# Context attention's softmax kept in its PSUM bank: scores plus side input written back, maxima and subtraction read there

## The chip, the cores and the metric

The kernel runs on one core of one Trainium2 chip. The metric is the device time of one execution in microseconds (us), the median of several runs. Durations of single instructions are in nanoseconds (ns) where marked.

## What is computed

Two layers on x of shape 4 x 1024 x 512, with a context of 4 x 64 x 512. The change lies in the first one, the attention over the context:

```python
qh = (q @ wq + bq).reshape(B, Lq, H, dk).transpose(0, 2, 1, 3)      # 16 heads of 64
kh = (k @ wk + bk).reshape(B, 64, H, dk).transpose(0, 2, 1, 3)
vh = (v @ wv + bv).reshape(B, 64, H, dv).transpose(0, 2, 1, 3)
scores = jnp.einsum('bhqd,bhkd->bhqk', qh / np.sqrt(dk), kh)
scores = scores + bias + graph_attn_bias        # both are the same input fside
weights = jax.nn.softmax(scores, axis=-1)       # over 64 context positions
ctx = jnp.einsum('bhqk,bhkd->bhqd', weights, vh)
out = layernorm(ctx @ wo + bo + q)
```

The second layer is a transformer block on that result: layer norm, self attention with 8-bit rounding of queries, keys, values and weights, attention over the context with the same rounding, and a gated feed-forward network of width 2048. Its code is not touched.

## The kernel before

The 4096 rows are worked on in eight chunks of 512 rows (n from 0 to 7), two chunks to a batch element; a chunk has NT = 4 tiles of 128 rows. For each batch element the kernel runs `cross` for both chunks, then `self_attention` and `middle` for each of them. The feed-forward network of a finished chunk is cut into 48 steps of twelve matmuls, and `feed` deals these out between the steps of later stages by hand-written plans; in `cross` of chunks 2 to 7 one such step comes ahead (slot 0) and the rest of that stage's share only in its tail, after the softmax steps. The last chunk's network runs alone at the end. Nothing is scheduled by the machine: every engine has its own program, in a fixed order, and they meet at semaphores.

A product of fp32 accuracy is made of three matmuls of high and low parts (`three`, lines 1724 to 1726): high x high, high x low, low x high. Four slices of the contraction make twelve matmuls of 512 columns.

For the context attention, setup has multiplied weights and context into per-batch matrices: M (x to scores) and N (probabilities to output). `cross(n)` has STEPS0 = 8 steps i: two halves of eight heads, by four row tiles. In step i, half h and tile t,

- TensorE computes the 128 x 512 scores (8 heads x 64 positions) in PSUM bank 0 (line 1952, matmuls at 1724 to 1726), after it waited until the bank's last content was emptied (line 1951); then it transposes the probabilities of step i - 2 into bank 1 (line 1959) and adds the output product of step i - 3 in banks 2 to 5 (line 1971).
- GpSimd adds the constant row crow to the side input fbias of a later step (line 929), makes low parts of M and N (line 901), and multiplies the exponents of step i - 2 by the reciprocal of their sum (line 951).
- VectorE: line 1549 computes 2 x fbias + scores, from SBUF and bank 0 into the SBUF buffer e (one of four), and signals the bank empty. Line 1553 takes the maxima over each head's 64 positions, and line 1556 subtracts them in place, both on e. Then follow sum and reciprocal of step i - 1 (lines 1562, 1564) and the low part of the transposed probabilities of step i - 2 (p_lo, helper line 1388).
- ScalarE takes the exponent of e in place once line 1556 is done (line 1263), and the high part of step i - 2's transposed probabilities (line 1271).
- SP loads the side input of step i into one of three fbias buffers (line 728); it waits until line 1549 of step i - 3 has read the buffer, which today is the same signal as "bank 0 emptied".

The order in which the banks are filled is written out in `bank_fills`. Semaphores `filled[bank]` and `emptied[bank]` count, and `wait_emptied` waits for the count of one fill. VectorE reaches its own next instruction through a semaphore too (`link`, `landed`), so each of the three instructions starts when the one before has ended.

The fills of bank 0 and 1 in `cross`, and the order of TensorE's step:

```python
for i in range(STEPS0):
    fills += [("s0", n, i, 0), ("p0T", n, i, 1)]
```

The other softmax over the context, in `middle`, reads 1024 scores from two banks: maxima at line 1658, subtraction from PSUM into SBUF at line 1661, sums of the SBUF result at line 1665.

Of the kernel before, what the change touches and what calls it, by code (L numbers as in the profile page):

```python
# [9 lines left out]
ALU = mybir.AluOpType  # L10
ACT = mybir.ActivationFunctionType
AX = mybir.AxisListType.X
# [3 lines left out]
SC = 64  # L16
# [13 lines left out]
STEPS0 = 2 * NT  # L30
# [229 lines left out]
def build(nc, a, out):  # L260

    ctx = ExitStack()
    with ctx:
# [6 lines left out]
        def signal(name, keys, by=1):  # L270
            return Signal(sem(name), keys, by)
# [38 lines left out]
        mx = [sb(f"row_max{i}", [P, H]) for i in range(2)]  # L310
# [80 lines left out]
        chunks = range(CHUNKS)  # L391
# [37 lines left out]
        w1T_used = signal("w1T_used", [(n, g) for n in chunks for g in range(UNITS // 4) if g % 4 < 3])  # L429
        xhi_done = signal("xhi_done", [(n, k) for n in chunks for k in range(KT)])  # L430
        fbias_ready = signal("fbias_ready", [(n, i) for n in chunks for i in range(STEPS0)])
        s0_ready = signal("s0_ready", [(n, i) for n in chunks for i in range(STEPS0)])
        e0_done = signal("e0_done", [(n, i) for n in chunks for i in range(STEPS0)])
        sum0_ready = signal("sum0_ready", [(n, i) for n in chunks for i in range(STEPS0)])
        p0_ready = signal("p0_ready", [(n, i) for n in chunks for i in range(STEPS0)])
# [37 lines left out]
        def bank(i):  # L473
            return psum[:, i, :]
# [6 lines left out]
        def wait_emptied(eng, key):  # L481

            i, n = FILL[key]
            eng.wait_ge(emptied[i], n + 1)
# [70 lines left out]
        def _(sp):  # L555
# [160 lines left out]
            def load_fbias(n, i):  # L716

                number = n * STEPS0 + i
                b, c = divmod(n, NC)
                half, t = divmod(i, NT)  # L720
                if i >= 3:
                    wait_emptied(sp, ("s0", n, i - 3))
                elif c > 0:
                    wait_emptied(sp, ("s0", n - 1, i - 3 + STEPS0))
                elif n > 0:
                    wait_filled(sp, ("a2", n - 1, NT - 1))
                q = c * CH + t * P
                sp.dma_start(fbias[number % 3][:], a["fside"][b, 8 * half:8 * half + 8, q:q + P, :].rearrange("h p s -> p h s")
                             ).then_inc(fbias_loaded[number % 3], 16)
# [356 lines left out]
        def _(act):  # L1086
# [156 lines left out]
            def cross(n):  # L1243

                def host(s):
                    if n >= NC:
                        feed(NC * (n // NC) - 1, FROM_A, A_SLOTS * (n % NC) + s)

                host(0)
                for k in range(KT):  # L1250
                    wait_filled(act, ("xT", n, k))
                    act.activation(ht_hi[:, k, :], bank(bank_of(("xT", n, k))), ACT.Copy).then_inc(xhi_done.sem, 1)
                if n == 0:
                    block_high((n, "M0"))
                block_high((n, "N0"))
                for i in range(STEPS0 + 2):
                    if i == 1:
                        block_high((n, "M1"))
                    if i == 5:
                        block_high((n, "N1"))  # L1260
                    if i < STEPS0:
                        act.wait_ge(s0_ready.sem, s0_ready.at((n, i)))
                        act.activation(e0[i % 4][:], e0[i % 4][:], ACT.Exp).then_inc(e0_done.sem, 1)
                    m = i - 2
                    if m >= 0:
                        wait_filled(act, ("p0T", n, m))
                        if 0 <= m - 2 < NT:
                            act.wait_ge(p0_used.sem, p0_used.at((n, m - 2)))
                        elif m - 2 >= NT:
                            wait_filled(act, ("o0", n, m - 2 - NT))  # L1270
                        act.activation(p0_hi[m % 2][:], bank(1), ACT.Copy).then_inc(phi_done.sem, 1)
                    host(1 + i)
                if n == 0:
                    for key in FIRST:
                        block_high(key)
                if n < NC:
                    prep_high(PREP_IN[n][0])
                for s in range(A_TAIL - 1, A_TAIL + NT):
                    host(s)
                norm_T("h1T", n, "L1_xattn_ln1_g", "L1_xattn_ln1_b", ht_hi)  # L1280
                host(A_TAIL + NT)
                host(A_TAIL + NT + 1)
                for i, kind in enumerate(("q1", "k1", "v1")):
                    for m in range(4):
                        quantise((kind, n, m), inv[:, i:i + 1])
                        if kind == "v1" and n % NC < NC - 1:
                            block_high((n + 1, "M0"), m, m)
                if n == 1:
                    prep_high(PREP_IN[n][1])
# [68 lines left out]
        def _(dve):  # L1358
            steps = [0]

            def link(ins):

                steps[0] += 1
                ins.then_inc(step, 1)
                return ins
# [18 lines left out]
            def emptied_bank(ins, key):  # L1384
                return ins.then_inc(emptied[bank_of(key)], 1)
# [145 lines left out]
            def cross(n):  # L1531
# [10 lines left out]
                for i in range(STEPS0 + 2):  # L1542
                    if i < STEPS0:
                        number = n * STEPS0 + i
                        key = ("s0", n, i)
                        e = e0[i % 4][:]
                        dve.wait_ge(fbias_ready.sem, fbias_ready.at((n, i)))
                        wait_filled(dve, key)
                        emptied_bank(dve.scalar_tensor_tensor(e.rearrange("p h s -> p (h s)"),  # L1549
                                                              fbias[number % 3][:].rearrange("p h s -> p (h s)"), 2.0,  # L1550
                                                              bank(0), ALU.mult, ALU.add), key)
                        wait_emptied(dve, key)
                        link(dve.tensor_reduce(mx[i % 2][:, 0:8], e, AX, ALU.max))
                        landed()
                        top = mx[i % 2][:, 0:8].rearrange("p (g o) -> p g o", o=1).broadcast_to((P, 8, SC))
                        dve.tensor_tensor(e, e, top, ALU.subtract).then_inc(s0_ready.sem, 1)
                    m = i - 1
                    if 0 <= m < STEPS0:
                        dve.wait_ge(e0_done.sem, e0_done.at((n, m)))
                        if m >= 2:  # L1560
                            dve.wait_ge(p0_ready.sem, p0_ready.at((n, m - 2)))
                        link(dve.tensor_reduce(rs[m % 2][:, 0:8], e0[m % 4][:], AX, ALU.add))
                        landed()
                        dve.reciprocal(rr[m % 2][:, 0:8], rs[m % 2][:, 0:8]).then_inc(sum0_ready.sem, 1)
                    m = i - 2
                    if m >= 0:
                        dve.wait_ge(phi_done.sem, phi_done.at((n, m)))
                        emptied_bank(lo_part(p0_lo[m % 2][:], bank(1), p0_hi[m % 2][:]), ("p0T", n, m))
                    host(1 + i)
# [579 lines left out]
```

## Time and profile before

| | |
|---|---|
| median of 3 runs | 3404.15 us |
| lowest, highest | 3402.14, 3405.04 us |
| span of the profiled execution | 3406.4 us, 50798 instructions |
| TensorE matmul busy | 2956.5 us, 87% |
| VectorE busy | 2099.8 us, 62% |
| GpSimd busy | 1772.2 us, 52% |
| ScalarE busy | 1669.4 us, 49% |
| DMA | 436.40 MB, mean 128 GB/s |

The profiled execution has no time of its own beside its span; the span is 2.25 us above the median of the runs.

How to read the rows: PE is TensorE's matmuls, PEld its weight loads, DVE VectorE, ACT ScalarE, POOL GpSimd, SP the engine that issues the transfers. L1549 is line 1549 of the kernel. An instruction is named by its line, what it writes and what it reads. In brackets stands the idle time of the engine just before it and what ended that idle time. Matmuls overlap in the pipeline, so their durations are longer than the distance from one to the next. PEclk is the granted clock of TensorE as a share of 2.4 GHz.

### The profile page before, as it was taken

The page shows a single profiled execution, that of the slowest core. Times are in us where ns is not written, and L with a number is a line of the kernel's source. Part 1 is how long each engine was busy: PE and PEld are TensorE (multiplying, and loading weights), DVE is VectorE, ACT ScalarE, POOL GpSimd, SP SyncE. Part 2 cuts the span into 40 slices and gives each one's busy share as a digit, 9 for nine tenths or more (in the row PEclk, how much of TensorE's full clock was granted, in tenths as well). Part 3 has the DMA queues.
Part 4 walks back from the last instruction along what each step waited for, and adds up shares of the span by engine and source line. Part 5 has one row for each costly group of instructions (what it writes and reads, how often), then busy time and mean ns, then how long its engine had stood idle before and what let it go on. Part 6 is the DMA issues. An engine that isn't in the chain of part 4 may idle for free.

```text
span 3406.4 us, 50798 instructions
## 1 busy us (share of the span) xinstructions
PE 2956.5 (87%) x19712; PEld 2148.8 (63%) x19712; DVE 2099.8 (62%) x3031; ACT 1669.4 (49%) x2690; POOL 1772.2 (52%) x1695
## 2 busy tenths in 40 slices
PE   7677686887899899799889899899988889889999
PEld 6555455556677657566667656656777646656777
DVE  4556585773666586685565586676565577677521
ACT  5332572873333475574333375475333276386321
POOL 3554573884545274575355185475365176376321
PEclk9888657898999899899999999899999989999999
DMA  8753103334443213324353313323353322232444
GB/s 276 220 200 133 56 1 133 108 119 179 162 164 141 91 63 125 130 88 155 130 176 111 123 51 141 126 74 135 133 188 99 142 75 100 97 120 75 171 152 160
DMA packets 199758, 436.40 MB, mean 128 GB/s; under 512 B 94944, under 2 KB 103392, under 8 KB 182368
## 3 DMA queue, kind: packets, MB, share of 16 engines
q1 hardware_dynamic: 199520, 433.15, 36.1%
q8 instruction: 158, 2.59, 0.3%
q14 instruction: 80, 0.66, 0.1%
HBM read 363.38 MB, written 65.54 MB: 126 GB/s over the span
## 4 chain that ended last, share of the span: by engine, by line
PE 60%; DVE 11%; POOL 11%; ACT 7%; issue 6%; DMA 2%; SPq 1%; POOLq 0%; DVEq 0%; ACTq 0%
PE psum L1724 17%; PE psum L1726 15%; PE psum L1725 15%; PE psum L2020 5%; POOL w1b L998 3%; PE psum L2008 3%; DVE mx L1612 2%; ACT e L1302 2%; PE psum L2034 2%; ACT psum L1189 1%; DVE w1T L1624 1%; POOL u_lo L1017 1%; POOL rec L993 1%; DMA fw_lo<-pieces 1%; POOL w_lo L901 1%
## 5 line engine op out<-in xcount | busy, mean ns | idle before, releaser
L1612 DVE TENSOR_REDUCE mx<-psum 128x1 f32<-128x1024 f32 x512 | 623.1, 1218 | 121.2 <-PE psum L2009 121.0
L998 POOL TENSOR_SCALAR w1b<-e,rec 128x1024 f16<-128x1024 f32 x512 | 574.7, 1122 | 138.6 <-PE psum L2020 66.3
L1302 ACT ACTIVATE e<-psum,nb,scale 128x1024 f32<-128x1024 f32 x512 | 617.5, 1206 | 19.8 <-POOL w1b L998 3.1
L1724 PE MATMUL psum<-h_hi,fw_hi 128*128 128x512 f32 x1024 | 464.9, 454 | 30.9 <-DVE h_lo L1388 10.0
L1624 DVE TENSOR_SCALAR w1T<-psum 128x1024 bf16<-128x1024 f16 x512 | 352.0, 687 | 176.4 <-PE psum L2020 163.6
L1725 PE MATMUL psum<-h_lo,fw_hi 128*128 128x512 f32 x1024 | 415.8, 406 | 0.0
L1726 PE MATMUL psum<-h_hi,fw_lo 128*128 128x512 f32 x1024 | 415.2, 405 | 0.0
L2020 PEld LDWEIGHTS psum<-ident,w1b 128*128 128x128 f16 x4096 | 260.7, 105 | 207.7 <-issue 127.7
L2020 PE MATMUL psum<-ident,w1b 128*128 128x128 f16 x4096 | 354.3, 236 | 40.2 <-DVE w1T L1624 21.1
L907 POOL TENSOR_TENSOR rstd<-ve,mhalf 128x1 f32<-128x1 f32 x128 | 86.8, 678 | 484.8 <-DVE ve L1494 484.8
L1724 PEld LDWEIGHTS psum<-h_hi,fw_hi 128*128 128x128 f32 x1024 | 199.6, 195 | 152.4 <-issue 99.4
L1486 DVE TENSOR_TENSOR x<-psum,x 128x512 f32<-128x512 f32 x224 | 152.3, 685 | 232.4 <-PE psum L1726 231.6
L1724 PE MATMUL psum<-w_hi,ht_hi 128*128 128x512 f32 x640 | 257.5, 402 | 20.2 <-DVE e L1549 13.7
L1017 POOL TENSOR_TENSOR u_lo<-gate,u_hi 128x512 fp32r<-128x512 f32 x128 | 164.7, 1289 | 202.6 <-ACT u_hi L1227 196.8
L1296 ACT ACTIVATE nb<-mx,nscale 128x1 f32<-128x1 f32 x512 | 149.6, 292 | 235.6 <-DVE mx L1612 227.1
L901 POOL TENSOR_TENSOR w_lo<-mixed,w_hi 128x512 fp32r<-128x512 f32 x140 | 189.5, 1376 | 132.0 <-ACT w_hi L1196 132.0
L1724 PE MATMUL psum<-fw_hi,u_hi 128*128 128x512 f32 x512 | 226.2, 442 | 31.2 <-POOL u_lo L1017 13.7
L1725 PE MATMUL psum<-w_lo,ht_hi 128*128 128x512 f32 x640 | 251.7, 393 | 0.0
L1726 PE MATMUL psum<-w_hi,ht_lo 128*128 128x512 f32 x640 | 251.3, 393 | 0.0
L1726 PEld LDWEIGHTS psum<-h_hi,fw_lo 128*128 128x128 f32 x1024 | 200.8, 196 | 47.2
L1134 ACT ACTIVATE qt<-psum,rounder,inv 128x512 f32<-128x512 f32 x128 | 99.9, 780 | 248.1 <-PE psum L1726 244.6
L2009 PE MATMUL psum<-k_odd,q_turned 32*128 32x512 bf16 x512 | 220.1, 431 | 0.0
(181 smaller groups left out, 6237.0 us busy)
## 6 DMA issues: line engine op xcount, KB each, us to landing
fw_hi<-pieces SPq DMA_DIRECT2D x168, 512.0 KB, 3.3
fw_lo<-pieces SPq DMA_DIRECT2D x168, 512.0 KB, 4.4
w_hi<-kept SPq DMA_DIRECT2D x45, 1024.0 KB, 4.9
w_lo<-kept SPq DMA_DIRECT2D x45, 1024.0 KB, 7.4
mixed<-mixed SPq DMA_DIRECT2D x32, 1024.0 KB, 5.4
fbias<-in_fside_Bx16xSxS SPq DMA_DIRECT2D x64, 256.0 KB, 3.2
unsplit<-in_L_xattn_ff_w SPq DMA_DIRECT2D x24, 512.0 KB, 5.1
pieces<-fw_hi SPq DMA_DIRECT2D x24, 512.0 KB, 2.7
```

The costliest lines, as they stand in the source:

```text
L901: pool.tensor_tensor(w_lo[s][:, k, :], w_mixed[s][:, k, :], w_hi[s][:, k, :].bitcast(F32), ALU.subtract).then_inc(block_lo_done.sem, 1)
L998: pool.tensor_scalar(w1b[u % NH][:], e1[u % NE][:], rec1[:, u % 8:u % 8 + 1], HALF, ALU.mult, ALU.add).then_inc(w1_ready.sem, 1)
L1017: pool.tensor_tensor(u_lo[:, m, :], gate[:, m, :], u_hi[:, m, :].bitcast(F32), ALU.subtract).then_inc(u_lo_done.sem, 1)
L1302: act.activation(e1[s % NE][:], psum[:, i:i + 2, :].rearrange("p i n -> p (i n)"), ACT.Exp, bias=nb1[:, s % 4:s % 4 + 1], scale=scale[:, 0:1],
L1486: return emptied_bank(dve.tensor_tensor(xt, bank(bank_of(key)), xt, ALU.add), key)
L1612: dve.tensor_reduce(mx1[:, s % 4:s % 4 + 1], psum[:, i:i + 2, :].rearrange("p i n -> p (i n)"), AX, ALU.max).then_inc(maxed1.sem, 1)
L1624: emptied_bank(dve.tensor_scalar(w1T[u % 8][:].rearrange("p k q -> p (k q)"), bank(bank_of(key)).bitcast(FP16), -HALF, W_HIGH, ALU.add, AL ...
L1724: pe.matmul(o, s_hi, m_hi, start=first, stop=False)
L1725: pe.matmul(o, s_hi, m_lo, start=False, stop=False)
L1726: return pe.matmul(o, s_lo, m_hi, start=False, stop=last)
L2009: ins = pe.matmul(bank(i + 1), q1_turned[turned, hg, t * P:t * P + P], k1[1][turned, hg, :], start=True, stop=True)
L2020: ins = pe.transpose(bank(bank_of(key)).bitcast(FP16)[:, k * P:k * P + P], w1b[u % NH][:, k * P:k * P + P], ident16[:])
```

## The change

Line 1549 writes its result back into bank 0 instead of e, and signals a semaphore of its own, fbias_added, that SP waits for before it reloads the fbias buffer. Maxima and subtraction read bank 0. The subtraction writes e and signals the bank empty; ScalarE's exponent waits for that signal. The semaphore s0_ready goes.

```diff
@@ -429,7 +429,7 @@
-        s0_ready = signal("s0_ready", [(n, i) for n in chunks for i in range(STEPS0)])
+        fbias_added = signal("fbias_added", [(n, i) for n in chunks for i in range(STEPS0)])
@@ -719,9 +719,9 @@
                 if i >= 3:
-                    wait_emptied(sp, ("s0", n, i - 3))
+                    sp.wait_ge(fbias_added.sem, fbias_added.at((n, i - 3)))
                 elif c > 0:
-                    wait_emptied(sp, ("s0", n - 1, i - 3 + STEPS0))
+                    sp.wait_ge(fbias_added.sem, fbias_added.at((n - 1, i - 3 + STEPS0)))
@@ -1259,7 +1259,7 @@
                     if i < STEPS0:
-                        act.wait_ge(s0_ready.sem, s0_ready.at((n, i)))
+                        wait_emptied(act, ("s0", n, i))
                         act.activation(e0[i % 4][:], e0[i % 4][:], ACT.Exp).then_inc(e0_done.sem, 1)
@@ -1546,14 +1546,14 @@
                         wait_filled(dve, key)
-                        emptied_bank(dve.scalar_tensor_tensor(e.rearrange("p h s -> p (h s)"),
-                                                              fbias[number % 3][:].rearrange("p h s -> p (h s)"), 2.0,
-                                                              bank(0), ALU.mult, ALU.add), key)
-                        wait_emptied(dve, key)
-                        link(dve.tensor_reduce(mx[i % 2][:, 0:8], e, AX, ALU.max))
+                        scores = bank(0).rearrange("p (h s) -> p h s", s=SC)
+                        dve.scalar_tensor_tensor(bank(0), fbias[number % 3][:].rearrange("p h s -> p (h s)"), 2.0,
+                                                 bank(0), ALU.mult, ALU.add).then_inc(fbias_added.sem, 1)
+                        dve.wait_ge(fbias_added.sem, fbias_added.at((n, i)))
+                        link(dve.tensor_reduce(mx[i % 2][:, 0:8], scores, AX, ALU.max))
                         landed()
                         top = mx[i % 2][:, 0:8].rearrange("p (g o) -> p g o", o=1).broadcast_to((P, 8, SC))
-                        dve.tensor_tensor(e, e, top, ALU.subtract).then_inc(s0_ready.sem, 1)
+                        emptied_bank(dve.tensor_tensor(e, scores, top, ALU.subtract), key)
```

## Rows read from the trace of the kernel before

**Rows 1.** The page's chain of work that ended last, by engine

```profile
PE 60%; DVE 11%; POOL 11%; ACT 7%; issue 6%; DMA 2%; SPq 1%; POOLq 0%; DVEq 0%; ACTq 0%
```

**Rows 2.** Line 1549: who waited for it (us, times)

```profile
  PE psum L1724: 13.7, 16
```

**Rows 3.** Line 1959: its engine sat idle before it until (us, times)

```profile
  POOL e L951: 28.7, 24
```

**Rows 4.** VectorE's groups of instructions: shapes, count, busy us, mean ns, idle before

```profile
L1556 DVE TENSOR_TENSOR e<-e,row_max 128x512 f32<-128x512 f32 x64 | 76.5, 1195 | 2.2
...
L1388 DVE TENSOR_TENSOR p_lo<-psum,p_hi 128x512 fp32r<-128x512 f32 x64 | 44.3, 692 | 42.8 <-ACT p_hi L1271 42.8
L1549 DVE SCALAR_TENSOR_TENSOR e<-fbias,psum 128x512 f32<-128x512 f32 x64 | 44.0, 687 | 94.5 <-PE psum L1726 90.7 <-POOL fbias L929 3.8
...
L1661 DVE TENSOR_TENSOR e<-psum,row_max 128x1024 f32<-128x1024 f32 x32 | 39.2, 1224 | 1.1
L1658 DVE TENSOR_REDUCE row_max<-psum 128x16 f32<-128x1024 f32 x32 | 38.9, 1215 | 10.3 <-PE psum L2080 9.6
L1665 DVE TENSOR_REDUCE row_sum<-e 128x16 f32<-128x1024 f32 x32 | 38.7, 1208 | 0.0
```

**Rows 5.** Line 1556: duration ns min/median/max, first and last start

```profile
L1556 DVE TENSOR_TENSOR e<-e,row_max x64: 691/1290/1828, 134.5 to 2647.1; 128x512 f32<-128x512 f32 x64
```

**Rows 6.** The third chunk's steps in order of time: start us, us, engine, line

```profile
924.68 0.69 DVE L1549 SCALAR_TENSOR_TENSOR e<-fbias,psum 128x512 f32<-128x512 f32 x1 [2.85 <-PE psum L1726]
...
925.42 0.50 PE L1724 MATMUL psum<-w_hi,ht_hi 128*128 128x512 f32 x1 [0.86 <-DVE e L1549]
...
926.12 0.77 DVE L1556 TENSOR_TENSOR e<-e,row_max 128x512 f32<-128x512 f32 x1
...
928.09 0.39 PE L1726 MATMUL psum<-w_hi,ht_lo 128*128 128x512 f32 x1
...
928.59 0.69 DVE L1549 SCALAR_TENSOR_TENSOR e<-fbias,psum 128x512 f32<-128x512 f32 x1 [1.70 <-PE psum L1726]
...
932.84 0.66 PE L1959 MATMUL psum<-ident,e 128*128 128x128 f32 x4 [0.47 <-POOL e L951]
...
938.05 0.65 PE L1959 MATMUL psum<-ident,e 128*128 128x128 f32 x4 [1.82 <-POOL e L951]
...
966.30 0.66 PE L1959 MATMUL psum<-ident,e 128*128 128x128 f32 x4 [1.16 <-POOL e L951]
```

**Rows 7.** First line 1549 and second transposes of chunks 0 and 1, by time

```profile
133.05 0.69 DVE L1549 SCALAR_TENSOR_TENSOR e<-fbias,psum 128x512 f32<-128x512 f32 x1 [7.49 <-PE psum L1726]
...
147.54 0.66 PE L1959 MATMUL psum<-ident,e 128*128 128x128 f32 x4 [1.77 <-POOL e L951]
...
247.62 0.69 DVE L1549 SCALAR_TENSOR_TENSOR e<-fbias,psum 128x512 f32<-128x512 f32 x1 [1.45 <-PE psum L1726]
...
261.61 0.66 PE L1959 MATMUL psum<-ident,e 128*128 128x128 f32 x4 [1.76 <-POOL e L951]
```

**Rows 8.** Two matmuls of chunk 0's first scores, six apart, at the half clock

```profile
128.64 0.63 PE L1725 MATMUL psum<-w_lo,ht_hi 128*128 128x512 f32 x1
...
131.20 0.63 PE L1725 MATMUL psum<-w_lo,ht_hi 128*128 128x512 f32 x1
```

**Rows 9.** TensorE's matmuls behind idle gaps of 1.79, 2.00 and 2.66 us

```profile
1109.88 0.50 PE L1724 MATMUL psum<-fw_hi,u_hi 128*128 128x512 f32 x1 [1.79 <-DMA fw_lo<-pieces]
...
1002.79 0.76 PE L1724 MATMUL psum<-ht_hi,w_hi 128*128 128x512 f32 x1 [2.00 <-DVE ht_lo L1388]
...
2670.51 0.47 PE L1724 MATMUL psum<-fw_hi,u_hi 128*128 128x512 f32 x1 [2.66 <-issue]
```

**Rows 10.** Stretches at those gaps: us, busy PE, PEld, DVE, ACT, POOL, PEclk, DMA

```profile
1110.00:1112.00 2.00, 2.00 (x11) 1.68 (x12) 0.00 (x0) 0.00 (x0) 0.00 (x0) 1.00 0.00 0
1002.00:1004.00 2.00, 1.21 (x3) 0.83 (x3) 1.33 (x2) 2.00 (x4) 0.00 (x0) 0.62 0.99 367
2670.00:2672.00 2.00, 1.49 (x6) 1.09 (x6) 0.70 (x3) 1.86 (x1) 0.55 (x1) 0.90 0.90 354
```

## The prediction

> **What bounds the kernel now.** I read the shares of the chain of waits first: TensorE has 60% of it [rows 1]. So a change counts where it lets TensorE start earlier or later. The change touches only the eight steps of the context attention's softmax in each of the eight chunks (64 steps of 3406 us). Next came the view of line 1549, which empties PSUM bank 0 today: 16 times, 13.7 us in all, TensorE sat idle until it ended, two times per chunk [rows 2]. TensorE's transposes of the probabilities (line 1959) waited 24 times, 28.7 us, for GpSimd's multiplication, three times per chunk [rows 3]. Last came the stretch of one chunk in order of time [rows 6], to see which of these waits hangs on which.
>
> In that stretch the scores of step 0 are in the bank, line 1549 runs from 924.68, and TensorE, idle 0.86 us, starts the scores of step 1 at 925.42 when the bank is free. The same happens at step 2. There is no other work for TensorE in steps 0 to 2: the first transpose belongs to step 0's probabilities, and it comes in its program after step 2's scores. It waits 0.47 us at 932.84 and the second one 1.82 us at 938.05 [rows 6]. From there TensorE has scores, transposes and output products in every step and waits no more until the seventh transpose. The second transpose's start is therefore the place where I measure the delay.
>
> **The vector work.** Per step there are three VectorE instructions: line 1549 with 687 ns, the maxima of 1553 about as long, and the subtraction of 1556 with 1195 ns [rows 4]. The subtraction is the odd one: it has two SBUF inputs and takes from 691 to 1828 ns [rows 5], and its mean is far above that of other 128x512 tensor_tensor rows with one PSUM input, 692 ns (the row of p_lo) [rows 4]. The subtraction of the other softmax, line 1661, reads PSUM as the changed one will, and takes 1224 ns for twice the elements. Half of 1224 with a fixed part gives about the 692 ns of p_lo, so I take 690 ns. The gain on VectorE is 64 x (1195 - 690) = 32.3 us of busy time. The maxima stay: reading PSUM takes 1215 ns against 1208 ns from SBUF for 128x1024 (lines 1658, 1665) [rows 4]. No row has VectorE writing PSUM; the nearest are the 687 ns of line 1549 itself, which already reads it, and 692 ns. I take 690 ns for it, with 70 ns less or more as bounds: ten times the 7 ns just named.
>
> The Trainium skill ("VectorE: DVE Perf Modes", the errata section and the rules for kernel authors) speaks against this change: it gives a fixed 120 cycles for a PSUM source and 58 for an SBUF source, and advises a copy to SBUF first where many operations read a result. By it maxima and subtraction would each cost some 0.065 us more, an estimate from that page, and the sum below would grow by 8 x 3 x 2 x 0.065 = 3 us. The trace has 7 ns for such a pair of rows, and the sum goes by the trace.
>
> **The wait that is added.** Today bank 0 is free at the end of line 1549; after the change at the end of the subtraction, two instructions later. Counting from the start T of step 0's line 1549, with pitches of 0.72 us as in the trace (924.68 to 926.12 for two) [rows 6]: the subtraction starts at T + 1.44 and ends at T + 2.13, TensorE starts at T + 2.18 instead of T + 0.74. Its burst of twelve matmuls lasts 3.06 us (925.42 to 928.48, the end of the matmul at 928.09) [rows 6], and the next line 1549 starts 0.11 later. So:
> - scores of step 1 end at T + 5.24, its subtraction at T + 7.48;
> - scores of step 2 run T + 7.53 to T + 10.59; first transposes then, with no wait, as they are released 4.25 us after step 1's line 1549 starts (928.59, that is 0.11 after 928.48, to 932.84), which then is T + 9.6;
> - step 2's subtraction ends at T + 12.83, so the scores of step 3 wait too, which they don't today; they run T + 12.88 to T + 15.94;
> - second transposes at T + 15.95. GpSimd is ready: its first and second multiplication release TensorE 5.21 us apart now (932.84 to 938.05, low parts and a bias sum between them) [rows 6], so at T + 14.8.
>
> Today the second transposes are at 938.05 = T + 13.37. The delay is 2.58 us, in the six chunks from the third on. In the first two GpSimd's queue makes them late already: 147.54 - 133.05 = 14.49 and 261.61 - 247.62 = 13.99 [rows 7], so 1.46 and 1.96 are added. Sum: 6 x 2.58 + 1.46 + 1.96 = **18.9 us**.
>
> From step 4 on the bank's longer use is hidden: TensorE has four transposes and twelve output products between two bursts of scores, the latter alone 2.67 us at the pitch above, and the vector chain needs 0.11 + 2.13. If that cover (at least 0.43 us) were gone, each of 4 steps a chunk would cost what is missing. The seventh transposes wait 1.16 us a chunk today (966.30) [rows 6] behind step 7's chain, whose subtraction already takes 0.69; nothing comes back there. The faster subtractions of steps 3 to 6 sit behind a busy TensorE and give nothing. ScalarE's exponent starts with the subtraction's end, as before. SP waits for the same instruction (1549) through another semaphore, so the side input's transfers, and what stands behind them in SP's queue (weights, pieces), move only with TensorE. GpSimd's bias sums wait for those transfers and stay early.
>
> **The clock.** The two idle gaps of 0.86 us become 2.29 us each (0.11 + 2.13 + 0.05), with a third of about the same length broken by transposes. Does TensorE's granted clock survive them? After a gap of 1.79 us between dense matmuls it stayed at 1.00 (2.4 GHz); after one of 2.66 us, also between dense matmuls, its mean over two us was 0.90, on the way to 0.50 (1.2 GHz); after one of 2.00 us beside transposes 0.62 [rows 9, 10]. Of 15 gaps from 2.00 (1002.79) to 2.66 us (2670.51) at the full clock I count 14 that were followed by a fall, most beside transposes or small matmuls; of 27 from 1.6 to below 2.00, 7. A gap of 2.29 lies 0.57 of the way from 1.79 to 2.66, so I take a fall in 5 of 8 chunks. Its price: at the half clock the pitch is (131.20 - 128.64) / 6 = 0.427 us [rows 8], at full 2.67 / 11 = 0.243 [rows 6]; eleven pitches of a burst cost 2.0 us more. 5 x 2.0 = **10 us**, bounds 0 (no fall) and 8 x 2 x 2.0 = 32 (both bursts in each chunk).
>
> The Trainium skill ("TensorE: Matmul & The Clock Gate", practices table) warns only of longer gaps between bursts than these. By it the clock term would be 0; the rows above disagree.
>
> **Sum**, against the median: 3404.15 + 18.9 + 10 = **3433 us**. The profiled execution spans 3406.4 us, 2.3 above that median; against it the same sum gives 3435.3. With the write and the reads at +-0.07 us, three gaps a chunk move it by 24 x 2 x 0.07 = 3.4.
>
> **Rivals.**
> - The clock holds everywhere: 3404.15 + 18.9 = 3423. For it: gaps of 1.79 and 1.82 did no harm. Chance 0.15.
> - The clock falls in both gaps of all chunks: 3404.15 + 18.9 + 32 = 3455. For it: 14 of 15. Against it: those were mostly beside sparse work. 0.12.
> - Part of the delay is absorbed downstream by something that doesn't follow TensorE, as GpSimd's queue does in the first chunk: 8 x 1.46 = 12, so 3416. 0.12.
> - All of it is absorbed, a transfer or GpSimd setting each chunk's end: 3404. Against it: TensorE's 60% of the chain. 0.05.
> - The subtraction still stretches beside GpSimd: it stays 0.5 us longer, three gaps a chunk: +12 on the forecast, 3445. The 692 and 1224 ns speak against it. 0.03.
> - It gets faster: bank 0 is not what TensorE waits for, the stretched subtraction of steps 0 and 1 is. Then the time above 0.69 in those comes off; 1.14 us is the most that one of them can give (1828 ns against 690) [rows 5], so at most 16 x 1.14 = 18 less, 3386. It decides if the scores of steps 1 and 2 start later than the bank comes free; today the burst at 925.42 follows line 1549 by 0.05 us [rows 6], so they don't. 0.03.
>
> **How the numbers follow.** The forecast has 0.50. A measurement of this kernel can tell about 0.2%, 6.8 us, from no change. Slower by more: all but the absorbed case and the faster one, 0.92. Within: 0.05. Faster: 0.03. The range leaves out the two last and the upper part of the dearest case: 3414 to 3447.
>
> **What would show it.** After the change line 1556 should be near 690 ns with no spread, 1549 and 1553 unchanged. TensorE's idle time in front of scores (ended by 1556) should be about 24 waits: 2.29 us twice and 1.5 to 1.9 once a chunk, some 48 us against 13.7; the first two waits of line 1959 should be gone and the seventh still be 1.16. The second transposes should start 15.95 us after the chunk's first line 1549. At those gaps the granted clock should read 0.5 in some chunks. I am wrong if the gaps are there and the end is not later (absorbed), or if the bank is free sooner than two instructions after 1549.

## The result, and the profile after

The changed kernel took 3453.7 us (median of four runs, 3445.98 to 3457.36); the kernel before, in four runs beside it, 3404.6 us (3402.14 to 3410.2). The ratio is 1.0144, 95% interval 1.0125 to 1.0162: slower, as forecast, but by 49 us where 29 were forecast, and above the range's upper end of 3447. The profiled execution of the changed kernel spans 3444.2 us, 37.8 more than the 3406.4 of before, and lies low among its own runs. A second session gave 3445.85 against 3403.32 us (below). So the size to be explained is 38 to 49 us, of which a trace can show its own 38.

The view of line 1556 (now the one that empties the bank) gives its durations and who waited for it:

```profile
L1556 DVE TENSOR_TENSOR e<-psum,row_max x64: 690/691/694, 136.9 to 2687.8; 128x512 f32<-128x512 f32 x64
...
  PE psum L1724: 52.5, 24
```

These are the subtraction's shortest, middle and longest duration in ns, then the time for which TensorE waited for it (us, times). Against [rows 5] the spread of the subtraction is gone. Against [rows 2] TensorE waits for the bank 24 times instead of 16, and 52.5 us instead of 13.7. VectorE's groups of instructions (shapes, count, busy us, mean ns, idle before), to be read against [rows 4]:

```profile
L1550 DVE SCALAR_TENSOR_TENSOR psum<-fbias,psum 128x512 f32<-128x512 f32 x64 | 44.6, 696 | 167.0 <-PE psum L1726 159.6 <-POOL fbias L929 7.4
...
L1553 DVE TENSOR_REDUCE row_max<-psum 128x8 f32<-128x512 f32 x64 | 44.2, 691 | 2.2
L1556 DVE TENSOR_TENSOR e<-psum,row_max 128x512 f32<-128x512 f32 x64 | 44.2, 691 | 2.2
```

VectorE's busy time fell from 2099.8 to 2067.5 us, the 32.3 forecast, and the kernel is slower all the same. The third chunk in order of time (start us, duration us; in brackets the idle time before and what ended it), against [rows 6]:

```profile
935.88 0.70 DVE L1550 SCALAR_TENSOR_TENSOR psum<-fbias,psum 128x512 f32<-128x512 f32 x1 [2.80 <-PE psum L1726]
...
937.34 0.69 DVE L1556 TENSOR_TENSOR e<-psum,row_max 128x512 f32<-128x512 f32 x1
...
938.08 0.50 PE L1724 MATMUL psum<-w_hi,ht_hi 128*128 128x512 f32 x1 [2.31 <-DVE e L1556]
...
945.00 0.50 PE L1724 MATMUL psum<-w_hi,ht_hi 128*128 128x512 f32 x1 [2.31 <-DVE e L1556]
...
949.45 0.60 PE L1959 MATMUL psum<-ident,e 128*128 128x128 f32 x4
...
951.92 0.50 PE L1724 MATMUL psum<-w_hi,ht_hi 128*128 128x512 f32 x1 [1.87 <-DVE e L1556]
...
956.37 0.60 PE L1959 MATMUL psum<-ident,e 128*128 128x128 f32 x4
...
984.53 0.66 PE L1959 MATMUL psum<-ident,e 128*128 128x128 f32 x4 [1.17 <-POOL e L951]
```

Three gaps, 2.31, 2.31 and 1.87 us, stand where two of 0.86 stood. The first two transposes don't wait any more, the seventh still waits. But the distance between the starts at 938.08 and 945.00 is 6.92 us: 2.31 of gap leaves 4.6 for twelve matmuls that take 3.06 in [rows 6]. The same stretch in windows (us, then busy time of PE, PEld, DVE, ACT and POOL, granted clock as a share of 2.4 GHz, DMA share, GB/s):

```profile
936.00:938.00 2.00, 0.00 (x0) 0.00 (x0) 1.93 (x3) 0.00 (x0) 2.00 (x3) 1.00 0.33 120
938.00:940.00 2.00, 1.92 (x6) 1.52 (x7) 0.03 (x1) 1.94 (x3) 0.80 (x1) 0.76 0.54 123
940.00:942.00 2.00, 2.00 (x6) 1.60 (x5) 0.00 (x0) 1.06 (x1) 0.00 (x0) 0.50 0.00 0
```

The granted clock fell from 2.4 to 1.2 GHz about a microsecond behind the end of the first long gap: 0.76 over 938 to 940 is 1.00 for half of it and 0.50 for the other half. I take the second transposes' start after the chunk's first sum (line 1550, before 1549) as the prediction did. For chunks 0 to 7 it is 18.24, 18.89, 20.49, 18.94, 17.32, 18.95, 18.94 and 18.83 us, together 150.6; before it was 14.49, 13.99, 13.37, 13.39, 13.31, 13.34, 13.38 and 13.37, together 108.6. The 42.0 us between the sums are the change's whole effect up to there, and by the eighth transposes it is still 41.3 (402.1 against 360.8): hardly anything is lost or won back in steps 3 to 7. The span's 37.8 is 4 less.

In windows from 2 us before to 20 us behind each chunk's first sum, the granted clock fell 15 times in the changed kernel, once to three times in each of the eight chunks, and stood 54.4 us at 1.2 GHz. In the kernel before it fell in none of them; only the last 1.0 us of an earlier stretch at 1.2 GHz reaches into the first window. Falls are counted in this way in all that follows. Outside these windows the time at 1.2 GHz varies from kernel to kernel without a pattern (545 us before, 521 after, 501 to 547 in others); I take the 4 us as part of that, which no run shows.

### The profile page after: what moved, and what is told of

It reads as the page before. It is cut to its first block, busy times and chain, and to the rows that moved or that the text cites. A ratio compares the mean times of both kernels' runs of the same rounds, so it can differ in the third digit from the quotient of the medians.

```text
span 3444.2 us, 50798 instructions
## 1 busy us (share of the span) xinstructions
PE 2970.7 (86%) x19712; PEld 2163.3 (63%) x19712; DVE 2067.5 (60%) x3031; ACT 1669.0 (48%) x2690; POOL 1753.9 (51%) x1695
## 4 chain that ended last, share of the span: by engine, by line
PE 61%; DVE 12%; POOL 9%; ACT 8%; issue 6%; DMA 2%; SPq 1%; POOLq 0%; DVEq 0%; ACTq 0%
PE psum L1724 18%; PE psum L1725 16%; PE psum L1726 16%; PE psum L2020 5%; POOL w1b L998 3%; PE psum L2008 3%; DVE mx L1612 2%; ACT e L1302 2%; PE psum L2034 2%; ACT psum L1189 2%; DVE w1T L1624 1%; POOL rec L993 1%; POOL u_lo L1017 1%; ACT ht_hi L1188 1%; DMA fw_lo<-pieces 1%
## 5 line engine op out<-in xcount | busy, mean ns | idle before, releaser
L1724 PE MATMUL psum<-w_hi,ht_hi 128*128 128x512 f32 x640 | 267.3, 418 | 59.0 <-DVE e L1556 52.5
L1725 PE MATMUL psum<-w_lo,ht_hi 128*128 128x512 f32 x640 | 261.5, 409 | 0.0
L1726 PE MATMUL psum<-w_hi,ht_lo 128*128 128x512 f32 x640 | 260.2, 407 | 0.0
L1724 PE MATMUL psum<-fw_hi,u_hi 128*128 128x512 f32 x512 | 226.5, 442 | 29.0 <-POOL u_lo L1017 13.7
L901 POOL TENSOR_TENSOR w_lo<-mixed,w_hi 128x512 fp32r<-128x512 f32 x140 | 177.8, 1294 | 131.8 <-ACT w_hi L1196 131.8
```

The lines of the kernel that those rows point to most:

```text
L901: pool.tensor_tensor(w_lo[s][:, k, :], w_mixed[s][:, k, :], w_hi[s][:, k, :].bitcast(F32), ALU.subtract).then_inc(block_lo_done.sem, 1)
L1724: pe.matmul(o, s_hi, m_hi, start=first, stop=False)
L1725: pe.matmul(o, s_hi, m_lo, start=False, stop=False)
L1726: return pe.matmul(o, s_lo, m_hi, start=False, stop=last)
```

## The experiments

There are two questions: is it the later release or the PSUM operands that cost, and how do the 42 us divide between waiting and clock? Nine edited kernels ran, and the changed kernel once more. Ratios are each against runs of the kernel before on the same chip, with 95% intervals.

**The useless matmuls in the gaps** (busy_gaps_after). The changed kernel, with 8, 8 and 6 matmuls into bank 7, which nothing reads, ahead of the scores of steps 1, 2 and 3. The wait for the bank stays, TensorE merely isn't idle in it.

```diff
+                        if i == 1:
+                            last = ("f", NC * (n // NC) - 1, 1 + 8 * (n % NC)) if n >= NC else ("f", 0, 1)
+                            pe.wait_ge(emptied[7], FILL[last][1])
+                        for _ in range({1: 8, 2: 8, 3: 6}.get(i, 0)):
+                            pe.matmul(bank(7), ht_hi[:, 0, 0:P], w_hi[SLOT[n, "M0"]][:, 0, :], start=True, stop=True)
                         wait_empty(key)
```

> The changed kernel, with matmuls of no use (8, 8 and 6 of 512 columns into the idle bank 7) in TensorE's three waits for the subtraction (steps 1, 2 and 3 of each chunk). The waits themselves stay, so the second transposes can't start earlier than 15.95 us after the chunk's first line 1549. Theory, wait plus clock: the granted clock stays at 1.00 in these stretches, the second transposes start 15.9 to 16.2 us after it in all eight chunks (17.3 to 20.5 in the changed kernel), and the time falls from 3453.7 to about 3404.6 + 18.9 = 3423, 3418 to 3430. Rival, the longer waits alone cost all of it and the clock is a by-product: the time stays at 3445 to 3458. Rival, the extra work of the useless matmuls counts: above 3454.

Measured: 3423.39 us (3420.95 to 3426.21), ratio 1.0066, 1.0053 to 1.0078; span 3419.2. The third chunk in order of time (its sum starts at 928.42), and its windows:

```profile
930.62 0.50 PE L1724 MATMUL psum<-w_hi,ht_hi 128*128 128x512 f32 x1 [0.51 <-DVE e L1556]
...
936.00 0.50 PE L1724 MATMUL psum<-w_hi,ht_hi 128*128 128x512 f32 x1 [0.51 <-DVE e L1556]
...
944.18 0.60 PE L1964 MATMUL psum<-ident,e 128*128 128x128 f32 x4
```

```profile
932.00:936.00 4.00, 3.49 (x17) 2.54 (x15) 2.14 (x4) 1.64 (x2) 0.71 (x1) 1.00 0.08 16
936.00:940.00 4.00, 4.00 (x20) 3.31 (x20) 1.57 (x4) 0.61 (x1) 3.05 (x3) 1.00 0.24 55
```

The pitch from one step's scores to the next is 5.38 us and the clock stays at 1.00 in every chunk. The second transposes come at T + 15.76 (944.18 - 928.42; the prediction's 15.95, with T for the first sum), in the other chunks at 15.70 to 15.79 and once at 16.11; the eight sum to 126.4. That divides the 42.0: 126.4 - 108.6 = 17.8 us is the wait, 150.6 - 126.4 = 24.2 us the clock. The bank is just as late as in the changed kernel, so more than half of the 42.0 us is not the wait itself but TensorE's slower work behind it. The division holds as far as useless matmuls change nothing else. In the medians the two parts come out a little differently: this kernel is 3423.39 against 3400.03 us, and the lower end of its ratio's interval, 1.0053, is 18 us. Some of that may be more than the 17.8 of the traces; no run says where it would arise.

**The control** (busy_gaps_before). The same in the kernel before, with 2, 2 and 0 matmuls in its 0.86 us gaps.

```diff
...
+                        for _ in range({1: 2, 2: 2, 3: 0}.get(i, 0)):
+                            pe.matmul(bank(7), ht_hi[:, 0, 0:P], w_hi[SLOT[n, "M0"]][:, 0, :], start=True, stop=True)
```

> Control for the useless matmuls: the kernel before with two of them in each of its two gaps of 0.86 us (steps 1 and 2). They fit into the gaps, whose granted clock is 1.00 already. Theory: no change within 0.2%; second transposes as in the kernel before (13.3 to 14.5 us after the chunk's first sum). Rival, extra activity of TensorE changes the clock elsewhere and was what saved the 30 us in busy_gaps_after: then this is faster than before too, by more than 0.3%.

Measured: 3399.15 us, ratio 0.9991, 0.9981 to 1.0002; sum of the second transposes 108.3 against 108.6. Useless matmuls alone bring nothing that can be told from noise where the clock holds anyway.

**The later release alone** (late_release_sbuf). The semaphores of the change (SP's and ScalarE's waits with them, left out below), but sum, maxima and subtraction stay in SBUF as before.

```diff
-                        emptied_bank(dve.scalar_tensor_tensor(e.rearrange("p h s -> p (h s)"),
-                                                              fbias[number % 3][:].rearrange("p h s -> p (h s)"), 2.0,
-                                                              bank(0), ALU.mult, ALU.add), key)
-                        wait_emptied(dve, key)
+                        dve.scalar_tensor_tensor(e.rearrange("p h s -> p (h s)"), fbias[number % 3][:].rearrange("p h s -> p (h s)"), 2.0,
+                                                 bank(0), ALU.mult, ALU.add).then_inc(fbias_added.sem, 1)
+                        dve.wait_ge(fbias_added.sem, fbias_added.at((n, i)))
...
-                        dve.tensor_tensor(e, e, top, ALU.subtract).then_inc(s0_ready.sem, 1)
+                        emptied_bank(dve.tensor_tensor(e, e, top, ALU.subtract), key)
```

> The kernel before, where only the signal that bank 0 is empty (and ScalarE's start) moves from the sum to the subtraction, as in the changed kernel; sum, maxima and subtraction stay in SBUF. Theory, the later release is the cause: as slow as the changed kernel or slower, since the subtraction in SBUF takes 690 to 1830 ns: gaps of 2.3 to 3.4 us, the clock falls in all chunks, 3450 to 3470. Rival, PSUM as target and source is what costs: near 3405 to 3415.

Measured: 3454.5 us (3453.01 to 3456.78), ratio 1.0158, 1.0144 to 1.0171; second transposes 155.3, 17 falls in all eight chunks, 59.0 us at 1.2 GHz there. The view of its subtraction:

```profile
L1555 DVE TENSOR_TENSOR e<-e,row_max x64: 691/966/1826, 137.1 to 2696.5; 128x512 f32<-128x512 f32 x64
...
  PE psum L1723: 56.3, 29
```

The release alone makes the kernel as slow as the whole change: the two intervals, 1.0144 to 1.0171 and 1.0125 to 1.0162, overlap. The second transposes sum to 4.7 us more, as the subtraction that now holds the bank still stretches (966 ns in the middle, up to 1826), and TensorE waits for it 29 times. The PSUM operands are not the cause.

**Only the sum in another bank** (sum_to_other_bank). The opposite part: line 1550 writes into bank 7 and releases bank 0 at once, as before; maxima and subtraction read bank 7.

```diff
+                        if number > 0:
+                            dve.wait_ge(s0_ready.sem, s0_ready.at((n, i - 1) if i > 0 else (n - 1, STEPS0 - 1)))
+                        scores = bank(7).rearrange("p (h s) -> p h s", s=SC)
+                        emptied_bank(dve.scalar_tensor_tensor(bank(7),
+                                                              fbias[number % 3][:].rearrange("p h s -> p (h s)"), 2.0,
+                                                              bank(0), ALU.mult, ALU.add), key)
...
+                        dve.tensor_tensor(e, scores, top, ALU.subtract).then_inc(s0_ready.sem, 1)
```

> The kernel before, where the sum goes to the idle bank 7 instead of SBUF and maxima and subtraction read it there; bank 0 is released by the sum, as before. This is the change without its longer hold of bank 0. Theory: the subtraction takes 0.69 us in all 64 steps (32 us less VectorE time), and little of it is on the path: second transposes 0 to 1 us earlier in the first two chunks, none later; 3401 to 3405, no change within 0.2%. Rival, the faster subtraction is worth its 32 us or a good part: below 3395. Rival, PSUM as target and source costs: above 3410.

Measured: 3396.53 us, ratio 0.9989, 0.9980 to 0.9997, no falls in the softmax stretches. The second transposes sum to 103.3, that is 5.3 us less than before: 1.1 to 1.3 us in each of the first two chunks, and some 0.5 in each of the others, where the expectation had nothing. The third chunk, whose first sum starts at 922.82, and two of GpSimd's groups:

```profile
935.70 0.66 PE L1962 MATMUL psum<-ident,e 128*128 128x128 f32 x4 [1.34 <-POOL e L951]
```

```profile
L901 POOL TENSOR_TENSOR w_lo<-mixed,w_hi 128x512 fp32r<-128x512 f32 x140 | 178.3, 1296 | 131.3 <-ACT w_hi L1196 131.3
...
L929 POOL TENSOR_TENSOR fbias<-fbias,crow 128x512 f32<-128x512 f32 x64 | 82.1, 1293 | 0.0
```

The second transposes now wait 1.34 us for GpSimd instead of 1.82 [rows 6] and come at T + 12.88 instead of 13.37. In the kernel before these two GpSimd groups had means of 1376 and 1409 ns. The time was lost beside the subtraction: in the kernel before, the w_lo and fbias instructions that run for over 0.1 us at the same time as line 1556 take 1466 and 1591 ns in the mean, all others 1303 and 1285, and 28 of these w_lo that run beside the sum or the maxima 1288. In the present kernel the same two groups are 1291 and 1297 ns beside the subtraction. So while the subtraction had two SBUF inputs, both engines were longer at their work; with one from PSUM neither is. The vector work that I counted as wholly hidden is worth some 4 us of the time (3396.53 against 3400.03), if the bank is free as early as before.

**A second bank for the scores** (two_banks_after, two_banks_before). Odd steps' scores go to bank 7 in the order of fills, which also needs the preceding feed-forward steps to be listed ahead of them (left out below); in the first on top of the change, in the second on the kernel before.

```diff
             for i in range(STEPS0):
-                fills += [("s0", n, i, 0), ("p0T", n, i, 1)]
+                fills += [("s0", n, i, (0, 7)[i % 2]), ("p0T", n, i, 1)]
...
-                        scores = bank(0).rearrange("p (h s) -> p h s", s=SC)
+                        scores = bank(bank_of(key)).rearrange("p (h s) -> p h s", s=SC)
```

> The changed kernel with the scores of odd steps in bank 7 instead of bank 0, so that TensorE needn't wait for the subtraction of the step before. Theory: the 24 waits and the falls of the clock in these stretches go. Scores of steps 0, 1 and 2 then run one after another; the first transposes wait for GpSimd until about 7.1 us after the chunk's first sum and the second until about 12.0 (13.37 in the kernel before). That is 1.4 us a chunk less than before: 3404.6 - 11 = 3394, 3385 to 3402. Rival, PSUM operands cost something by themselves: above 3405.

> The kernel before, with the scores of odd steps in bank 7: sum, maxima and subtraction stay in SBUF. Against two_banks_after (3393.3, 0.9971 of before) it tells what reading PSUM is worth once the bank is no bottleneck. Theory: the wait of 0.86 us goes twice a chunk, but the second transposes hang on GpSimd, whose low parts and VectorE's subtraction slow each other down while both read SBUF: second transposes at 12.2 to 13.5 us, time between before and two_banks_after, 0.998 to 1.000 of before. Rival, PSUM operands bring nothing: as fast as two_banks_after, 0.997.

Measured: on the change 3393.3 us (3383.88 to 3394.82), ratio 0.9971, 0.9960 to 0.9983; on the kernel before 3395.9 us, ratio 0.9983, 0.9973 to 0.9992. Second transposes 95.3 and 102.3. The third chunk of the first (its sum at 920.55), then its line of subtraction and that of the second:

```profile
927.53 0.66 PE L1965 MATMUL psum<-ident,e 128*128 128x128 f32 x4 [1.66 <-POOL e L957]
...
932.27 0.65 PE L1965 MATMUL psum<-ident,e 128*128 128x128 f32 x4 [1.32 <-POOL e L957]
```

```profile
L1562 DVE TENSOR_TENSOR e<-psum,row_max x64: 691/691/693, 134.7 to 2634.1; 128x512 f32<-128x512 f32 x64
```

```profile
L1562 DVE TENSOR_TENSOR e<-e,row_max x64: 691/1321/1828, 136.6 to 2639.8; 128x512 f32<-128x512 f32 x64
```

No score waits for a bank now, in either kernel, and the loss of 1.3 to 1.4% is gone: with the change the kernel is 0.3% faster than before, without it 0.2%. Whether the change itself adds anything to the second bank can't be told, as these two intervals overlap. The second transposes are 7.0 us earlier with it, but only some 0.45 us in four of the eight chunks, as in the run before. In three others the two-bank kernel without the change has a fall of the clock ahead of its second transposes (with the change, one does), so part of the 7.0 is the clock. One of the three is the third chunk, whose first sum starts at 923.85:

```profile
931.28 0.66 PE L1965 MATMUL psum<-ident,e 128*128 128x128 f32 x4 [2.11 <-POOL e L957]
```

```profile
930.00:932.00 2.00, 0.72 (x5) 0.69 (x6) 1.93 (x4) 0.00 (x0) 1.82 (x2) 1.00 0.09 21
932.00:934.00 2.00, 2.00 (x7) 1.54 (x6) 1.81 (x3) 0.95 (x2) 2.00 (x2) 0.55 0.49 110
```

Here the clock fell 0.9 us behind the end of one gap of 2.11 us.

**Sum and reciprocal first** (two_banks_sum_first). With two banks the transposes wait for GpSimd, GpSimd for the reciprocal. So, on top of two_banks_after, sum and reciprocal of step i - 1 go ahead of line 1550 of step i.

```diff
+                    m = i - 1
+                    if 0 <= m < STEPS0:
+                        dve.wait_ge(e0_done.sem, e0_done.at((n, m)))
+                        if m >= 2:
+                            dve.wait_ge(p0_ready.sem, p0_ready.at((n, m - 2)))
+                        link(dve.tensor_reduce(rs[m % 2][:, 0:8], e0[m % 4][:], AX, ALU.add))
+                        landed()
+                        dve.reciprocal(rr[m % 2][:, 0:8], rs[m % 2][:, 0:8]).then_inc(sum0_ready.sem, 1)
                     if i < STEPS0:
...
```

The same lines go from their place behind line 1550's block.

> two_banks_after, with VectorE's sum and reciprocal of step i - 1 ahead of step i's three instructions instead of behind them. In two_banks_after TensorE still waits for GpSimd's multiplication 1.66, 1.32 and about 1.17 us a chunk, and that multiplication waits for these sums. Theory: the first and the seventh transposes come 1 to 2.2 us earlier up to TensorE's own limit, the second by about 1.5 as GpSimd's chain starts earlier: 8 x (1.2 + 1.2) = 19 us, 3393 - 19 = 3374, 0.990 to 0.994 of before. Rival, the new order makes each step's sum late and TensorE waits for bank or exponent instead: no faster than 3393.

Measured: 3390.74 us (3383.16 to 3397.26), ratio 0.9966, 0.9953 to 0.9979, not to be told from two_banks_after and not the 0.990 to 0.994 that I expected. The wait only changed its owner:

```profile
933.16 0.63 PE L1965 MATMUL psum<-ident,e 128*128 128x128 f32 x4 [2.63 <-DVE p_lo L1394]
```

The multiplication is earlier, but the low part p_lo of the step before is now behind more vector work, and the second transposes wait for it instead, 2.63 us against 1.32. Behind this gap, the longest in the softmax steps of that chunk, the granted clock held:

```profile
933.00:937.00 4.00, 3.84 (x19) 3.28 (x20) 2.78 (x6) 1.08 (x2) 4.00 (x4) 1.00 0.39 100
```

Of the six chunks that have such a gap of some 2.6 us here, it held in three and fell in three.

**How long a gap the clock bears** (trimmed_gaps_after, half_gaps_after). The same insertion as in the first experiment, with other numbers: 2, 2 and 0 matmuls leave gaps of 1.86 us, shorter than the 2.31 of the change and like the 1.82 us in [rows 6] that did no harm before; 5, 5 and 3 leave 1.18.

```diff
-                        for _ in range({1: 8, 2: 8, 3: 6}.get(i, 0)):
+                        for _ in range({1: 2, 2: 2, 3: 0}.get(i, 0)):
```

> The changed kernel with only two useless matmuls in the waits of steps 1 and 2 and none in step 3: the idle gaps shrink from 2.31 us to about 1.8, the release of the bank stays. Theory, the idle length decides over the clock and 1.8 us is short enough (gaps of 1.79 and 1.82 stayed at the full clock in the kernel before): clock 1.00 in most of the 16 gaps, second transposes at 15.7 to 16.1 us in at least six chunks, time 3423 to 3430 against a kernel before of 3400 to 3405. Rival, what counts is how much TensorE works over the whole stretch: the clock still falls in half of the chunks or more, above 3433.

> The changed kernel with 5, 5 and 3 useless matmuls in the waits of steps 1, 2 and 3: idle gaps of about 1.15 us instead of 2.31 (full, 8, 8, 6: clock held in all chunks; trimmed, 2, 2, 0, gaps of 1.86: it fell in all chunks). Theory, there is a limit between the two and 1.15 lies on the good side, as 0.86 does in the kernel before: clock 1.00, second transposes at 15.7 to 16.1 us, time 1.005 to 1.008 of before. Rival, three gaps in a row of any length over a microsecond are too many: falls in half of the chunks, above 1.009.

Measured: trimmed 3445.53 us (3435.74 to 3446.94), ratio 1.0122, 1.0102 to 1.0141; half 3423.58 us (3416.83 to 3425.63), ratio 1.0062, 1.0048 to 1.0076. The third chunk of the trimmed kernel, in order of time and in windows:

```profile
936.69 0.50 PE L1724 MATMUL psum<-w_hi,ht_hi 128*128 128x512 f32 x1 [1.86 <-DVE e L1556]
...
943.61 0.50 PE L1724 MATMUL psum<-w_hi,ht_hi 128*128 128x512 f32 x1 [1.84 <-DVE e L1556]
```

```profile
936.00:938.00 2.00, 1.31 (x5) 1.02 (x6) 0.64 (x1) 1.33 (x3) 1.37 (x2) 0.85 0.59 135
938.00:940.00 2.00, 2.00 (x6) 1.61 (x5) 0.00 (x0) 1.68 (x1) 0.00 (x0) 0.50 0.00 0
```

And of the half one:

```profile
931.79 0.50 PE L1724 MATMUL psum<-w_hi,ht_hi 128*128 128x512 f32 x1 [1.18 <-DVE e L1556]
...
937.13 0.50 PE L1724 MATMUL psum<-w_hi,ht_hi 128*128 128x512 f32 x1 [1.18 <-DVE e L1556]
```

```profile
930.00:934.00 4.00, 2.82 (x13) 2.01 (x12) 1.67 (x3) 2.23 (x3) 2.48 (x3) 1.00 0.35 89
934.00:938.00 4.00, 2.82 (x13) 2.03 (x12) 2.87 (x5) 1.42 (x2) 0.00 (x0) 1.00 0.28 64
```

The trimmed kernel's clock fell in all eight chunks (18 times, 61.8 us, second transposes 153.8), the half one's in none (126.4, the very sum of busy_gaps_after). My expectation of the first was wrong and what its rival forecast came true: 1.86 us is enough here, though waits of 1.76 to 1.83 in seven chunks of the kernel before were not. It isn't needed that such gaps repeat: in five of the eight chunks the first fall came by the first gap, before the second had begun. The windows above show it for the third chunk, where the clock is at 0.50 from 938 on and the second gap ends at 943.61. So neither the length of a gap nor the number of gaps decides alone, and my count by length could not have given the answer. The runs change the gaps and TensorE's work around them together; what does decide stays open.

**The changed kernel again** (changed_again), on the chip and beside the runs of half_gaps_after, with no edit.

> The changed kernel as it is, timed beside the others. The second transposes account for 42 us in the profiled execution, the medians for 49. Theory, the difference of 7 us is the granted clock in other stretches, which varies from run to run: 1.012 to 1.015 of before, median 41 to 51 us above it. Rival, a cost outside the softmax steps: always 47 or more above before.

Measured: 3445.85 us (3444.75 to 3449.91), ratio 1.0131, 1.0114 to 1.0147; 17 falls, 58.8 us, second transposes 152.5. Against it half_gaps_after is 22.3 us faster in the medians and 152.5 - 126.4 = 26.1 in the traces' sums. So the useless work in the gaps gives back the clock's part, on the same chip too.

## Why the prediction was right and wrong

**The direction and its mechanism: right.** The bank is free two vector instructions later; late_release_sbuf has only that and is as slow. TensorE's new waits are those forecast: 2.31 us twice and 1.87 once a chunk (forecast 2.29 and 1.5 to 1.9), 24 waits with 52.5 us (forecast about 48). The first two waits of line 1959 are gone and the seventh is 1.17 us (1.16). That the PSUM operands have no part in it is shown from the other side by sum_to_other_bank, which has them all and is not slower.

**The wait's term: right.** 18.9 us were forecast and 17.8 measured with the clock held, T + 15.76 against 15.95. The cover from step 4 on held, since the changed kernel is behind by 42.0 us at the second transposes and by 41.3 at the eighth. So next to nothing was absorbed downstream, and the rivals in which part (3416) or all (3404) of it is are refuted.

**The clock's term: the step that failed.** It was "I take a fall in 5 of 8 chunks", at 10 us; it measured 24.2. The clock fell in all eight, and in six of them two or three times: 15 falls. The price of one was nearly right, 24.2 / 15 = 1.6 us against the 2.0 put on it. The fault lay in the count. I placed 2.29 us between one gap that did no harm and one that did, and I took one fall a chunk at most where the chunk has three such gaps in a row. The trimmed kernel shows that even gaps of 1.86 us bring a fall in every chunk, the half kernel that 1.18 does not; and gaps of 2.6 us, in the kernel with the sum first, brought one in three chunks of six. So the step that read a chance off the length between two single gaps had no ground. The rival in which the clock falls in both gaps of all chunks, 3455 and put at 0.12, is the nearest to what happened, dear by 8 us in its clock term (32 against 24.2); that its 3455 lies so near the 3453.7 of the first session is in part luck. The 14 falls behind 15 gaps of the prediction's own count spoke for it, and I set them aside for being mostly beside sparse work. (Counting falls up to 3.5 us behind the gap's end, the trace gives 13 for these 15 gaps, and 9 for 29 gaps from 1.6 to below 2.00 us where the prediction has 7 of 27; this changes nothing in the argument.) With the measured terms the sum is 3404.15 + 17.8 + 24.2 = 3446, beside 3445.85 in the second session. That the first session's median is 8 us more is not explained by any run; its lowest run, 3445.98, which is the profiled one, is at the sum.

The Trainium skill ("TensorE: Matmul & The Clock Gate", practices table) warns only of longer gaps, and by it the clock term would have been 0; the traces disagree, with falls behind 2.31 us and behind 1.86 us.

**The vector work: the size right, its effect nearly so.** Line 1556 came out at 691 ns with no spread (690), the maxima at 691, line 1550 writing PSUM at 696 (690, with 70 either way as bounds): 32.3 us less busy time. By the Trainium skill ("VectorE: DVE Perf Modes", the errata section) a PSUM source would be dearer by some 65 ns, the prediction's estimate from that page; the trace disagrees: the maxima cost 691 ns from PSUM here and 686 from SBUF in late_release_sbuf, 5 ns more. "The faster subtractions give nothing" was a little wrong. With the release kept early they bring the second transposes 0.5 us earlier in most chunks, 5.3 us in all, through GpSimd, whose own instructions are no longer slowed beside the subtraction (1297 ns for fbias there against 1591).

**The rival of a faster kernel (3386): wrong for the change**, since the scores follow the bank's release and not the subtraction. What does beat the kernel before is a second bank for the scores: 3393.3 us with the change, 3390.74 with the sum first as well, 3395.9 without the change. These three can't be told apart by their intervals. That the second bank is what helps is shown; that the change is worth keeping on top of it is not.

## What to carry to other kernels

Before moving a chain of operations into a PSUM bank, count how many instructions later the bank comes free and who fills it next; either give the next fill another bank or copy out with the first operation. Price a new idle gap on TensorE twice, as its length and as the half-speed matmuls behind it. Here gaps of 1.2 us were safe and gaps of 1.9 us and more mostly not, but the length alone did not decide: take the fall in every chunk as the dear end of the range, and test it. Where the gap can't be closed, filling it with matmuls that nobody reads shows the clock's part, and gives it back.

## What was not expected of the hardware

- The granted clock fell in 8 of 8 chunks with gaps of some 1.86 us, in five of them before the second gap had begun, and held in all 8 at 1.18 us; in the kernel before it held behind waits of 1.76 to 1.83 us in seven chunks. In two other kernels it fell behind one gap of 2.11 us and held behind one of 2.63 us.
- Filling half of a gap was as good as filling nearly all of it: gaps of 1.18 us and of 0.51 us gave the same sum of 126.4 us and 3423.58 and 3423.39 us.
- The subtraction with two SBUF inputs slows GpSimd as well as itself: GpSimd's fbias instructions took 1591 ns in the mean beside it and 1285 away from it; with one input from PSUM they took 1297 beside it.
- A VectorE sum written to PSUM costs 696 ns for 128x512 against 687 into SBUF.
